# State scan: uneven groups of 3, 3, 3, 3, 2 and 2 weighed states in place of four groups of 4

## The reference, cut to what matters

```python
def step(state, xs):
    d_t, B_t, C_t, u_t = xs
    dA = jnp.exp(d_t[..., None] * A)
    state = state * dA + (d_t * u_t)[..., None] * B_t[:, None, :]
    y_t = jnp.einsum('ben,bn->be', state, C_t)
    return (state, y_t)
```

## Time and profile before

| | |
|---|---|
| median of 3 runs | 2528.97 us (2526.53 to 2531.1) |
| the profiled execution's own time | 2532.93 us |
| its span | 2531.1 us |
| TensorE busy in the span | 2178.9 us (86%) |
| VectorE busy | 1774.3 us (70%) |
| GpSimd busy | 1083.8 us (43%) |
| ScalarE busy | 932.2 us (37%) |
| granted TensorE clock, mean | 0.936 of full |
| the stage with the scan | about 1235 to 1820 us |

### The profile page before, as it was taken

The page is one execution under the profiler, slowest core; times in us unless marked ns, Lnnn a source line. Parts: engine busy times, 40 slices in busy tenths (PEclk is TensorE's granted clock), DMA queues, the critical chain, the costliest instruction groups (busy, mean ns, idle before and its releaser), DMA issues. The chain is left out here.

```text
span 2531.1 us, 25434 instructions
## 1 busy us (share of the span) xinstructions
PE 2178.9 (86%) x7344; PEld 1121.6 (44%) x7344; DVE 1774.3 (70%) x2992; ACT 932.2 (37%) x1772; POOL 1083.8 (43%) x805
## 2 busy tenths in 40 slices
PE   6998998999899967675489898999589999999848
PEld 2544544555455533332355555555233333334234
DVE  1887688778768867777488988988636464554454
ACT  1443333343333324333364645556113232232310
POOL 2454333335434314545589898999500000000033
PEclk9999999999999988877699999999779999999879
DMA  6000000000000031334853645443222122221021
GB/s 250 18 22 18 17 21 21 21 17 17 21 18 22 22 108 69 142 143 161 304 172 123 205 141 191 170 161 143 71 79 62 40 50 50 50 50 38 13 103 51
DMA packets 95550, 214.80 MB, mean 85 GB/s; under 512 B 15824, under 2 KB 33104, under 8 KB 93024
## 3 DMA queue, kind: packets, MB, share of 16 engines
q1 hardware_dynamic: 77184, 156.18, 18.9%
q10 hardware_dynamic: 17760, 57.42, 6.5%
q0 software_dynamic: 512, 0.13, 0.0%
HBM read 146.30 MB, written 42.07 MB: 74 GB/s over the span
## 5 line engine op out<-in xcount | busy, mean ns | idle before, releaser
L706 POOL TENSOR_SCALAR a_prob<-a_prob,a_rsum 128x256 f32<-128x256 f32 x256 | 147.1, 593 | 466.2 <-DVE a_rsum L634 466.0
L1342 DVE TENSOR_TENSOR_SCAN s_state<-s_decay,s_state 128x512 f32<-128x512 f32 x256 | 305.0, 1212 | 12.8 <-ACT s_decay L1284 12.5
L1298 POOL TENSOR_TENSOR s_state<-s_b_rows,s_delta_u 128x1024 f32<-128x1024 f32 x128 | 303.4, 2382 | 16.8 <-DMA s_b_rows<-scan_bc 14.4
L1460 PE MATMUL c_bank<-c_xn_parts,c_w_parts 128*128 128x512 f32 (+1 forms) x1056 | 271.9, 408 | 1.5 <-DVE c_xn_parts L1536 1.4
L1284 ACT ACTIVATE s_decay<-s_delta,s_a 128x512 f32<-128x512 f32 x256 | 173.6, 690 | 220.3 <-DVE s_state L1342 219.7
L2006 POOL DMA_DIRECT2D d_qs<-d_neg_t x16 | 8.2, 514 | 515.5 <-DVE d_neg_t L1937 515.5
L438 PE MATMUL a_bank<-a_xn_t,a_wq 128*128 128x512 f32 x512 | 227.2, 592 | 0.0
L1460 PEld LDWEIGHTS c_bank<-c_xn_parts,c_w_parts 128*128 128x128 f32 (+1 forms) x1056 | 197.8, 188 | 62.3 <-issue 14.2
L521 PE MATMUL a_bank<-a_wo,a_out_t 128*128 128x512 f32 x512 | 222.3, 592 | 0.0
L549 ACT ACTIVATE a_prob<-a_score,a_neg_m 128x256 f32<-128x256 f32 x256 | 117.9, 475 | 275.5 <-DVE a_neg_m L629 275.3
L1858 ACT ACTIVATE d_prob_t<-d_score 128x512 f32<-128x512 f32 x256 | 139.0, 595 | 194.5 <-PE d_score L1741 193.5
(11 more groups left out here) (197 smaller groups left out, 3764.5 us busy)
## 6 DMA issues: line engine op xcount, KB each, us to landing
s_b_rows<-scan_bc SPq DMA_DIRECT2D x64, 512.0 KB, 3.8
c_w_parts<-ffn_weights_hi ACTq DMA_DIRECT2D x39, 512.0 KB, 3.7
c_w_parts<-ffn_weights_lo ACTq DMA_DIRECT2D x39, 512.0 KB, 4.6
f_idx<-in_idx SPq DMA_DIRECT2D x64, 130.0 KB, 2.1
ffn_weights<-f_picks SPq DMA_DIRECT2D x64, 130.0 KB, 1.8
r_factor<-in_factors SPq DMA_DIRECT2D x8, 1024.0 KB, 8.1
d_qs<-d_hi SPq DMA_DIRECT2D x128, 64.0 KB, 2.0
d_ks<-d_hi SPq DMA_DIRECT2D x128, 64.0 KB, 2.0
```

Of the source, the lines that this page charges most:

```text
L1298: pool.tensor_tensor(self.state[:, s], row.broadcast_to([P, 2, T]), self.delta_u[:, h % 2], ALU.mult) \
L1342: dve.tensor_tensor_scan(self.state[:, s, e, :], self.decay[u % 2][:], self.state[:, s, e, :], 0.0, ALU.mult, ALU.add).then_inc(self.scann ...
L1460: mm = nc.tensor.matmul(banks[b][0:width[o], :], w_parts[:, n % SLOTS, w, at:at + width[o]], xn_parts[:, x_, k, :], start=((k, w, x_) == t ...
```

## The change

The groups of a half now hold 3, 3, 3, 3, 2 and 2 steps. A group of n steps still takes n - 1 additions, so a half has 10 in place of 12, and all of the scan 80 in place of 96. TensorE sums six group tiles for each half in place of four: 48 in place of 32, two matmuls each. A sum still stands three steps behind the last step of its group: in a pass at steps 0, 2, 5, 8, 11, 14, 16, 18, 21, 24, 27 and 30 (in the first pass from 5 on) in place of 2, 6, 10, 14, 18, 22, 26 and 30 (in the first from 6 on). The waits are counted anew from a table of the sizes. Slots, tiles, banks and transfers stay as they are.

```diff
-    GROUPS = N // 4
+    SIZES = (3, 3, 3, 3, 2, 2)
+    PER_HALF = len(SIZES)
+    GROUPS = 2 * B * PER_HALF
...
+    def adds_through(self, c):
+
+        g, n = self.group_of(c)
+        return c + 1 - (g + 1)
...
     def sum_group(self, pe, g):
-        h = g // 4
-        if g % 4 == 0 and h:
+        h, k = divmod(g, self.PER_HALF)
+        if k == 0 and h:
             pe.wait_ge(self.y_taken, 2 * h)
-        pe.wait_ge(self.gathered, 3 * g + 3)
+        pe.wait_ge(self.gathered, self.adds_through(self.last_of(g)))
...
-                                       start=(g % 4 == 0), stop=(g % 4 == 3))
+                                       start=(k == 0), stop=(k == self.PER_HALF - 1))
...
     def tensor(self, pe, c):
         if c + 1 < self.N:
             self.spread_c(pe, c + 1)
-        if c % 4 == 2 and c >= 6:
-            self.sum_group(pe, (c - 6) // 4)
+        g, n = self.group_of(c - 3) if c >= 3 else (0, 0)
+        if c >= 3 and c - 3 == self.last_of(g):
+            self.sum_group(pe, g)
 
     def tensor_end(self, pe):
-        self.sum_group(pe, self.GROUPS - 1)
+        for g in range(self.GROUPS):
+            if self.last_of(g) > self.N - 1 - 3:
+                self.sum_group(pe, g)
...
-            pool.wait_ge(self.gathered, 3 * (old // 4) + max(old % 4, 1))
+            g, n = self.group_of(old)
+            pool.wait_ge(self.gathered, self.adds_through(old + 1 if n == 0 else old))
...
     def gather(self, pool, c):
-        g, n = c // 4, c % 4
+        g, n = self.group_of(c)
...
-            pool.wait_ge(self.gathered, 3 * g + n - 1)
+            pool.wait_ge(self.gathered, self.adds_through(c - 1))
...
     def take_y(self, dve, h):
         dve.wait_ge(self.y_in, (h + 1) * 16)
-        dve.wait_ge(self.summed, 4 * h + 4)
+        dve.wait_ge(self.summed, self.PER_HALF * (h + 1))
```

More of the change, by code:

```diff
@@ L1184, in __init__, with group_of, last_of @@
         self.y_taken = core.sem("s_y_taken")
+    def group_of(self, c):
+        h, n = divmod(c, 16)
+        for g, size in enumerate(self.SIZES):
+            if n < size:
+                return h * self.PER_HALF + g, n
+            n -= size
+    def last_of(self, g):
+        h, k = divmod(g, self.PER_HALF)
+        return 16 * h + sum(self.SIZES[:k + 1]) - 1
+    def adds_through(self, c):
+        g, n = self.group_of(c)
+        return c + 1 - (g + 1)
     def sync_setup(self, sp):
```

## The result

The changed kernel is slower by 0.4%: 2540.39 us (median; 2535.48 to 2542.87) against 2530.54 (2526.53 to 2534.09), a ratio of 1.0039 with a 95% interval of 1.0028 to 1.0049. The prediction said 2527.7 us, within 2519 to 2540, most likely no change. The profiled execution took 2542.87 us, its span 2541.1, 10.0 more than before.

A forecast was written before the change was run, and what follows sets the result against it. It took a VectorE - TensorE - VectorE chain, in fills also VectorE - ScalarE - VectorE, to set the pace. Terms 2.3 + 4.2 - 3.6 - 2.6 - 1.6 = -1.3 us gave a 2527.7 us median, range 2519 to 2540 us.

The forecast's parts named there:

- GpSimd's part: Scan stage: 16 additions go, 38.1 us of GpSimd busy time; nobody waits for them, so 0 us gained.
- sign of error: VectorE's waits for TensorE at lifts grown by over 10 us would show the prediction wrong.
- The rival's partial form: Fills: TensorE partly the bound, +0.8 us at steps 5, 11, 14, 16, 18, +14 us; chance 0.13, wholly or in part.
- TensorE's part: Scan stage: 16 more sums of 1.71 us each, 27.4 us, priced by where they fall and how they change clock gaps.
- Plain fills and down pieces: Added or moved sums at these steps fit into TensorE's period or existing waits: 0 us.
- Step 5: Passes 0 to 2: the sum there delays the lift of piece 8 by 0.76 us, three times, +2.3 us.
- Step 7: Passes 0 to 2: gap grows from 2.17 to 3.3 us, half clock behind it, 1.4 us passed on each, +4.2 us.
- Step 24: Gap of 3.30 us shrinks to 1.59 us, full clock behind it: -1.2 us, three times, -3.6 us.
- Last pass: Gap of 2.79 us shrinks to 1.08; steps 25 to 26 take 3.67 us in place of 6.23: -2.6 us.
- Pass 0, piece 14: Step 10's half-clock sum goes, so the lift's 2.33 us wait falls to ScalarE's 0.73: -1.6 us.
- The last addition of y: End of the stage: left at 0; gain up to 1.7 us if the sum before it kept the clock up.
- The clock's rule: TensorE's clock halves behind gaps of 2.43, 2.79 and 3.30 us, not behind one of 2.17 us.

The follow-up runs named there:

- e5_pool_off: Changed kernel, GpSimd's power for the next norm one piece earlier and GpSimd waiting at piece 12 until all four normalisation operations are done: 2527.7 us, 0.9984 of before.
- e2_tensor_part: Kernel before, its groups and GpSimd additions kept, with TensorE's changed order and two added sums of zeroes in a half: 2529.0 us, 0.9996 of before.
- e6_pool_off_fill: e5_pool_off plus a TensorE sum of zeroes ahead of each of two gaps (steps 7 and 10) in passes 0 to 2: 2518.7 us, 0.9958 of before.

## Why the prediction was wrong

**The step that failed** is "Nobody waits for them (0.2 us in the stage), so the term is 0" of GpSimd's part. Nobody does wait, by the wait rows of after. But the reasoning took a wait as the only way in which an engine can cost another something. GpSimd's operation keeps some of VectorE's from running, and this shows as a longer operation. The Trainium skill, "SBUF — State Buffer", has it under "SBUF: two separate sides": the two engines share a port pair, taken as an exclusive lock for a whole instruction, by VectorE in a two-port mode (which a copy or tensor_scalar within SBUF can enter) or, where GpSimd's instruction reads SBUF, with two inputs there; the second to come stands still until the first is done. The traces agree for L190 (0.54 to 2.3 us under a GpSimd operation of 2.4 us) and L182; the scans and weighings, which read one side from PSUM, kept their times. The step also priced the edit as a count of additions. What mattered was which step has none: it moved from 8 to 9 and took two feeds with it. The term, put at 0 with bounds of 0.2 and 38.1 us to the good, was 14 us to the bad by e5_pool_off (10.9 of it in the stage), and no rival had it.

**Its sign of error worked.** VectorE's waits for TensorE at lifts grew by 14.6 us, which the text would have taken for TensorE as the bound. The rival's partial form, 2543 us, came near by accident: e2_tensor_part has TensorE's whole new order and stays at 0.9996.

**Terms of TensorE's part**, third pass by the trace:
- Plain fills and down pieces: 0, held.
- Step 5: the lift of piece 8 waits 0.69 us; +0.76 a pass, held.
- Step 7: half clock came as said, and the sum at step 8 gave +1.31 us for 1.4. What was left out is the fill behind step 7, +0.67 us at the lift of piece 10. The gap became 3.90 and not 3.3 us, 0.6 of it L182's.
- Step 24: the gap shrank as said, to 1.92 us, and in the second and third pass the clock fell one piece later. In the first pass it was worth -0.81 us, in the third +0.86, for -1.2 predicted each: the largest mis-sized term, -3.6 us that came to nothing. (In the second pass it was +0.77.)
- Last pass: -2.9 us for -2.6, held.
- Pass 0, piece 14: half of the gain came, the wait falling from 2.33 to 1.59 us. But it is 1.59, 1.34 and 1.59 us in the three passes, where before it was 0.67 and 0.68 in the second and third: the gap ahead of step 10 grew and the fill behind it runs at half clock. That is +0.7 and +0.9 us that no term had.
- The last addition of y: "left at 0; ... up to one sum's price, 1.7 us". The handover is 1.6 us shorter.
- The clock's rule: the prediction took gaps above 2.4 us as those behind which the clock falls. Its own trace has a fall behind a gap of 2.12 us, ahead of step 10 in the first pass (the sum there took 3.13 us in place of 1.88), and none behind the same gap in the next pass:

```profile
1291.87 0.50 PE L1242 MATMUL s_c<-s_c_parts,s_c_pick 128*128 128x512 f32 x1 [2.12 <-DVE s_state L1350]
1292.21 3.13 PE L1251 MATMUL s_y<-s_group,ident 128*128 128x512 f32 x4
```

- The range: its lower bound is given as "-9 us with the end", but the terms as listed give -7.2. The measured time is at the other end, so nothing hangs on it.

By the trace the stage is 11.9 us longer, the handover 1.6 shorter. With GpSimd's part harmless it is 1.0 (e5) or 4.0 us longer (e2), where the terms had said -1.3; the rest, 8 to 11 us, is put down to GpSimd's part.

**What to try.** e6_pool_off_fill beats both: 0.42% under the kernel before, 0.8% under the changed one.

## What to carry to other kernels

An engine that nobody waits for can still cost: compare the duration of each group of instructions, not only the waits, and look at which of VectorE's operations run wholly in SBUF and what GpSimd does beside them. When a change removes work from GpSimd, ask where the remaining work lands, not how much went; a wait that holds GpSimd for some 5 us in each of three passes was worth 14 us here. And an experiment that moves one engine's work moves the collisions of the others too, so put the suspected collision in by itself, and in a harmless place as its control.

## What the runs showed of the hardware

- A tensor_scalar of VectorE, SBUF to SBUF in fp32, took 0.54 us alone and up to 2.6 beside one of GpSimd's of 2.4 us. bn_stats, which also reads and writes SBUF, did not: 676 to 686 ns in all twelve cases before and 674 to 683 after, though in the third pass after GpSimd ran without a break over its four.
- The granted clock fell behind gaps of 3.62 and 3.90 us, and near the transposes behind one of 1.92 and one of 0.57 us close together in the second and third pass, not in the first. In the kernel before it fell behind a gap of 2.12 us in the first pass and stayed at 1.00 behind the same gap in the second and third. So the length of the single gap did not decide it, contrary to what the prediction had assumed. Twelve matmuls in three passes that add zeroes kept it up (47 to 12 us of half clock on the changed kernel).
